# Products of ones ahead of the first weights, modulation rows at the end of the first block, and the gate product split around the gate logits

## The reference, cut to what matters

```python
mod = (silu(c) @ wmod).reshape(2, 6, 1, 256)
sa, ca, ga, sb, cb, gb = (mod[:, i] for i in range(6))
ga, gb = sign(ga) * max(abs(ga), 0.25), sign(gb) * max(abs(gb), 0.25)
h = layernorm(x) * (1 + ca) + sa
q, k, v = h @ Wq, h @ Wk, h @ Wv
gk = log_sigmoid(h @ Wg1 @ Wg2 + bg2) / 16          # cumulated over each chunk of 64
...
o = o * rsqrt(mean(o * o) + EPS) * norm_w * silu(h @ Wgate)
x = x + ga * (o @ Wo)
h = layernorm(x) * (1 + cb) + sb
x = x + gb * moe(h)
```

## Time and profile before

| | us |
|---|---|
| median of three executions | 387.04 |
| their range | 384.47 to 387.41 |
| the profiled execution, its own time | 386.04 |
| its span, first to last instruction | 384.2 |
| mean granted TensorE clock | 0.994 |

### The profile page before, as it was taken

One profiled execution on the slowest core, in us unless ns is written; L12 is line 12 of the kernel. 1 busy time (PEld: TensorE's weight loads), 2 busy tenths in 40 slices (PEclk: granted clock), 3 DMA queues, 4 the chain that ended last, 5 costly groups with the idle time before them and its releaser, 6 DMA issues.

```text
span 384.2 us, 9939 instructions
## 1 busy us (share of the span) xinstructions
PE 359.4 (94%) x3837; PEld 224.8 (59%) x3838; DVE 239.4 (62%) x578; ACT 144.4 (38%) x303; POOL 146.2 (38%) x252
## 2 busy tenths in 40 slices
PE   2989989997989899699999999999999999999996
PEld 2445655674556556554864564576666666666464
DVE  3068767796778878945286483236555555555386
ACT  3395718642846350335023311113333333332110
POOL 7504203500240062005544046540667777675300
PEclk9999999998999999999999999999999999999999
DMA  7960300000000000039931045242233333311296
GB/s 251 309 201 2 114 3 3 2 5 3 1 2 3 3 2 3 4 114 333 292 101 62 1 113 136 90 140 57 83 112 100 108 102 98 99 56 43 83 352 229
DMA packets 29901, 36.66 MB, mean 95 GB/s; under 512 B 4567, under 2 KB 26530, under 8 KB 29860
## 3 DMA queue, kind: packets, MB, share of 16 engines
q1 hardware_dynamic: 26452, 27.58, 23.9%
q0 software_dynamic: 3408, 8.51, 6.5%
HBM read 23.31 MB, written 13.68 MB: 96 GB/s over the span
## 4 chain that ended last, share of the span: by engine, by line
PE 85%; ACT 6%; DVE 4%; issue 3%; DMA 1%; SPq 0%; DVEq 0%; ACTq 0%
PE at_ps L1815 13%; PE work L1445 10%; PE at_ps L1445 8%; PE work L1494 6%; PE at_ps L1460 6%; PE work L1838 4%; PE work L1460 3%; PE work L1840 3%; PE work L1681 2%; PE work L1631 2%; PE at_ps L1494 2%; PE at_ps L1799 2%; PE at_ps L1528 2%; PE at_ps L1681 2%; PE o_even L1584 1%
## 5 line engine op out<-in xcount | busy, mean ns | idle before, releaser
L656 POOL DMA_INDIRECT ys_tokens<-er_pos,goal_u x39 | 41.8, 1073 | 33.8 <-DVE er_pos L1368 25.6
L1815 PE MATMUL at_ps<-arena 128*128 x156 | 54.5, 472 | 0.0
L627 POOL DMA_INDIRECT xs_sorted<-h2tok,pos_u x32 | 31.8, 993 | 36.9 <-DVE pos_u L992 18.6
L585 POOL TENSOR_TENSOR sq<-sq,sg 128x512 f32<-128x512 f32 x8 | 10.0, 1271 | 92.6 <-issue 92.6
L1815 PEld LDWEIGHTS at_ps<-arena 128*128 128x128 f32 x156 | 26.6, 190 | 14.9 <-issue 6.6
L898 ACT ACTIVATE arena<-at_ps 128x176 f32<-128x176 f32 x39 | 12.4, 317 | 58.8 <-PE at_ps L1815 58.8
L1368 DVE SCALAR_TENSOR_TENSOR er_pos<-work,goal,sq 128x256 f32<-128x256 f32 x39 | 17.2, 480 | 22.0 <-PE work L1845 21.0
L1445 PE MATMUL work<-h2T,sup_sb 128*128 128x512 f32 x56 | 25.7, 598 | 0.0
L1348 DVE TENSOR_TENSOR arena<-at_ps,arena 128x176 f32<-128x176 f32 x39 | 13.3, 341 | 18.4 <-ACT arena L898 15.9
L1195 DVE COPY_PREDICATED arena<-causal,at_ps 128x512 f32<-128x512 uint32 x32 | 20.5, 719 | 5.8 <-PE at_ps L1528 5.8
L1460 PE MATMUL at_ps<-sdn_sb,hs 128*128 128x256 f32 x100 | 22.1, 380 | 0.0
(11 more groups left out here) (281 smaller groups left out, 815.6 us busy)
## 6 DMA issues: line engine op xcount, KB each, us to landing
h2tok<-xs_sorted SPq DMA_DIRECT2D x40, 131.5 KB, 2.1
arena<-ys_tokens SPq DMA_DIRECT2D x8, 512.0 KB, 7.8
arena<-in_e_up SPq DMA_DIRECT2D x8, 352.0 KB, 5.5
x_sb<-in_x SPq DMA_DIRECT2D x4, 512.0 KB, 6.9
out_rows<-x_sb SPq DMA_DIRECT2D x16, 128.0 KB, 4.2
sup_sb<-in_s_up SPq DMA_DIRECT2D x2, 640.0 KB, 4.7
xs_sorted<-state SPq DMA_DIRECT2D x2, 526.0 KB, 15.2
xs_sorted<-state SPq DMA_DIRECT2D x8, 131.5 KB, 3.8
```

Source lines behind the costliest of these rows:

```text
L627: g.indirect_dma_start(out=xs_dram, out_offset=bass.IndirectOffsetOnAxis(ap=pos_u[:, k, t:t + 1], axis=0), in_=h2tok[:, t, :], in_offset=N ...
L656: g.indirect_dma_start(out=ys_dram, out_offset=bass.IndirectOffsetOnAxis(ap=goal_u[:, i:i + 1], axis=0), in_=yout[:, q % 2, u, :], in_offs ...
L1815: ins = t_.matmul(at_ps[2 + u % 2][:, 0:2 * FE], xT[:, u % 2, k * P:(k + 1) * P], eup[:, bass.ds(e, 1), k, :].rearrange("p a n -> p (a n)" ...
```

## The change

- TensorE does 14 matmuls of a 128 x 128 tile of ones with itself into `at_ps0` before it waits for the modulation weights, and 3 more behind the first transposes (`idle_products`). Nobody reads their result. GpSimd writes `ones` first and raises the new semaphore `ones_ready` for them.
- `mod_rows` moves on TensorE from behind the low-rank product to between Q and V's second half in slot 0. ScalarE's eviction of it moves from behind `tT` to between the rows of block 1 and V's second half. Their 1024 KB of weights move on SP behind `wq`.
- G of block 0: its first half stands before the gate logits, its second half behind them. TensorE's wait for `const_pool` is gone.
- Banks: MODC goes to `at_ps2`, and of block 0 V's first half to `at_ps0` and K's first half to `at_ps1` (`FIRST_BANKS`), which nobody holds at that time.

```diff
@@ -67,15 +67,19 @@
          ("LR", 0): 3, ("WO", 1): 1, ("Z", 0): 2, ("Z", 1): 3}
 
 
+FIRST_BANKS = {("V", 0): 4, ("K", 0): 5}
+
+
 TAIL_BANKS = {1: (3, 2), 2: (4, 5), 3: (0, 1), 4: (3, 2), 5: (4,)}
 
 
 def unit_order():
-    units = [(("MODC", 0, 0), 0)]
+    units = [(("MODC", 0, 0), 2), (("XT", 0, 0), BANKS["XT", 0]), (("XT", 0, 1), BANKS["XT", 1])]
     ring = [2]
 
     def put(kind, blk, j):
-        units.append(((kind, blk, j), BANKS[kind, j]))
+        own = FIRST_BANKS if blk == 0 else {}
+        units.append(((kind, blk, j), own.get((kind, j), BANKS[kind, j])))
 
     def turn(*keys):
         for key in keys:
@@ -88,12 +92,16 @@
         for kind, blk, i in FILL.get((s, place), ()):
             part(kind, blk, i)
 
-    for kind, j in (("XT", 0), ("XT", 1), ("LR", 0), ("Z", 0), ("Z", 1)):
-        put(kind, 0, j)
+    put("LR", 0, 0)
+    put("G", 0, 0)
+    put("Z", 0, 0)
+    put("Z", 0, 1)
+    put("G", 0, 1)
     for s in range(NBLK):
         b, h = s - 1, s - 2
-        put("G", s, 0)
-        put("G", s, 1)
+        if s:
+            put("G", s, 0)
+            put("G", s, 1)
         put("V", s, 0)
         if h >= 0:
             put("HT", h, 0)
@@ -330,6 +338,7 @@
             sem(n) for n in ("ld_c", "ld_mod", "ld_wg", "ld_wgate", "ld_wv", "ld_wk", "ld_wq",
                              "ld_wo", "ld_rout", "ld_sh", "ld_ex"))
         xs_zero = sem("xs_zero")
+        ones_ready = sem("ones_ready")
         const_pool, ident_ready, zero_ready, kv_full = sem("const_pool"), sem("ident_ready"), sem("zero_ready"), sem("kv_full")
         modf_ready, mod_stored, ld_rows = sem("modf_ready"), sem("mod_stored"), sem("ld_rows")
         unit_full, modr_full, nmr_ready, ld_modr = sem("unit_full"), sem("modr_full"), sem("nmr_ready"), sem("ld_modr")
@@ -421,8 +430,6 @@
             sp.dma_start(csb[:, :, :], cT).then_inc(ld_c, 16)
             sp.dma_start(wmod_sb[:, :, 0:2 * HID], wmod.rearrange("(k p) n -> p k n", p=P)[:, :, 0:2 * HID]
                          ).then_inc(ld_mod, 16)
-            sp.dma_start(wmod_sb[:, :, 2 * HID:6 * HID], wmod.rearrange("(k p) n -> p k n", p=P)[:, :, 2 * HID:6 * HID]
-                         ).then_inc(ld_modr, 16)
             sp.wait_ge(zero_ready, 4)
             sp.dma_start(wg1_sb[:, :, 0:LOWR], wg1.rearrange("(k p) n -> p k n", p=P)).then_inc(ld_wg, 16)
             for j in range(NPAIR):
@@ -433,6 +440,8 @@
             for w_sb, w, s in ((wgate_sb, wgate, ld_wgate), (wv_sb, wv, ld_wv), (wk_sb, wk, ld_wk),
                                (wq_sb, wq, ld_wq)):
                 sp.dma_start(w_sb[:, :, :], w.rearrange("(k p) n -> p k n", p=P)).then_inc(s, 16)
+            sp.dma_start(wmod_sb[:, :, 2 * HID:6 * HID], wmod.rearrange("(k p) n -> p k n", p=P)[:, :, 2 * HID:6 * HID]
+                         ).then_inc(ld_modr, 16)
             for i in range(1, NBLK):
                 sp.dma_start(x_sb[:, i * TPB:(i + 1) * TPB, :],
                              x[i * BLK:(i + 1) * BLK, :].rearrange("(t p) c -> p t c", p=P)).then_inc(ld_x[i], 16)
@@ -515,6 +524,7 @@
         def _(pool):
             g = nc.gpsimd
             steps = Steps(pool, pool_step)
+            g.memset(ones[:, :], 1.0).then_inc(ones_ready, 1)
             g.memset(wg1_sb[:, :, :], 0.0).then_inc(zero_ready, 1)
             g.memset(wg2_sb[:, :], 0.0).then_inc(zero_ready, 1)
             g.memset(rout_sb[:, :, :], 0.0).then_inc(zero_ready, 1)
@@ -524,7 +534,7 @@
             steps.sync()
             g.affine_select(out=ident[:, :], in_=ident[:, :], compare_op=ALU.not_equal, fill=1.0,
                             base=0, pattern=[[-1, P]], channel_multiplier=1).then_inc(ident_ready, 1)
-            for m in (ones, tri, bd16, causal):
+            for m in (tri, bd16, causal):
                 steps.did(g.memset(m[:, :] if m is not causal else m[:, :, :], 1.0 if m is not bd16 else 1.0 / HEAD))
             steps.did(g.memset(rowreset[:, :, :], 1.0))
             steps.did(g.memset(esil[:, :, FE:ODD0], 0.0))
@@ -814,7 +824,6 @@
             act.wait_ge(modc_ready, 2)
             evac_xT(0)
             evac_low_rank(0)
-            evac_mod_rows()
             z_abs(0)
             for s in range(NBLK + 1):
                 b, h = s - 1, s - 2
@@ -864,6 +873,8 @@
                     silu_tables()
                     fill(s, "norm")
                 if s < NBLK:
+                    if s == 0:
+                        evac_mod_rows()
                     evac_v(s, 1)
                     for gr in range(KC):
                         wait_unit(act, ("KT", s, gr))
@@ -1496,19 +1507,25 @@
                 ins.then_inc(unit_full, 1)
 
 
-            pe.wait_ge(csil_ready, 1)
-            pe.wait_ge(ld_mod, 16)
-            o = begin(("MODC", 0, 0))
-            for w in range(2):
-                for h in range(KC):
-                    for k in range(KC):
-                        c0 = w * HID + h * P
-                        ins = t_.matmul(o[:, (w * KC + h) * BATCH:(w * KC + h + 1) * BATCH], wmod_sb[:, k, c0:c0 + P],
-                                        csil[:, k, :], start=(k == 0), stop=(k == KC - 1))
-            ins.then_inc(unit_full, 1)
-            pe.wait_ge(csilb_ready, 1)
+            def idle_products(n):
+
+                for _ in range(n):
+                    t_.matmul(at_ps[0][:, 0:P], ones[:, :], ones[:, :], start=True, stop=True)
+
+            def mod_cols():
+                pe.wait_ge(csil_ready, 1)
+                pe.wait_ge(ld_mod, 16)
+                o = begin(("MODC", 0, 0))
+                for w in range(2):
+                    for h in range(KC):
+                        for k in range(KC):
+                            c0 = w * HID + h * P
+                            ins = t_.matmul(o[:, (w * KC + h) * BATCH:(w * KC + h + 1) * BATCH], wmod_sb[:, k, c0:c0 + P],
+                                            csil[:, k, :], start=(k == 0), stop=(k == KC - 1))
+                ins.then_inc(unit_full, 1)
 
             def mod_rows():
+                pe.wait_ge(csilb_ready, 1)
                 pe.wait_ge(ld_modr, 16)
                 for k in range(KC):
                     for w in range(4):
@@ -1516,8 +1533,6 @@
                                         wmod_sb[:, k, (w + 2) * HID:(w + 3) * HID], start=(k == 0), stop=(k == KC - 1),
                                         skip_group_check=True)
                 ins.then_inc(modr_full, 1)
-
-            pe.wait_ge(ident_ready, 1)
 
             def score(n, q, j):
 
@@ -1699,20 +1714,24 @@
                                             start=True, stop=True)
                 ins.then_inc(kv_full, 1)
 
+            pe.wait_ge(ones_ready, 1)
+            idle_products(14)
+            pe.wait_ge(ident_ready, 1)
+            mod_cols()
             transpose_x(0)
+            idle_products(3)
             pe.wait_ge(ld_wg, 16 * (NPAIR + 3))
             low_rank(0)
-            mod_rows()
+            pe.wait_ge(ld_wgate, 16)
+            project(("G", 0, 0), wgate_sb, 0, hT)
             gate_logits(0)
-            pe.wait_ge(const_pool, 1)
+            project(("G", 0, 1), wgate_sb, 1, hT)
             for s in range(NBLK + 1):
                 b, h = s - 1, s - 2
                 if b >= 0:
                     pe.wait_ge(kh_ready, 2 * b + 2)
                     pe.wait_ge(qeo_ready, 4 * b + 4)
-                if s < NBLK:
-                    if s == 0:
-                        pe.wait_ge(ld_wgate, 16)
+                if 0 < s < NBLK:
                     for gr in range(KC):
                         project(("G", s, gr), wgate_sb, gr, hT)
                 if b >= 0:
@@ -1762,6 +1781,8 @@
                         pe.wait_ge(ld_wq, 16)
                     for gr in range(KC):
                         project(("Q", s, gr), wq_sb, gr, hT)
+                    if s == 0:
+                        mod_rows()
                     values(s, 1)
                     key_rows(s)
                 if s + 1 < NBLK:
```

## The result

The changed kernel takes 383.28 us (median of 19 executions, 380.0 to 385.79), the kernel before 387.03 (19 executions, 384.47 to 389.03). The ratio is 0.9906 with a 95% interval of 0.9882 to 0.9931: 3.75 us, or 0.9%, faster. The forecast was 382.0 with a range of 380.2 to 385.6. The sign and the place were right, the size was 1.3 us too large.

A forecast was written before the change was run, and what follows sets the result against it. TensorE, busy 94% of the span, and its feeding chains bound the kernel. Head 3.45 + hand-over 1.95 - eviction 0.4 = 5.0 us; 386.04 - 5.0 = 381.0, raised by 1.0 toward the median: 382.0, range 380.2 to 385.6.

The forecast's parts named there:

- Fourteen products: TensorE ahead of MODC: the products of ones end by about MODC's weight landing at 6.84, costing 0 to 0.3 us.
- Rival D: TensorE's queue before MODC: products overrun at 0.47 us a pass, some 6 us slower, 393; chance 0.06.
- MODC warm: First modulation matmuls on TensorE: 16 passes at the raised clock take some 1.85 instead of 3.54 us, saving 1.7.
- Low rank: Block 0's low-rank product on TensorE at the raised clock: 1.11 instead of 1.93 us, saving 0.8.
- Gate logits: Block 0's gate logits on TensorE at the raised clock: 1.13 instead of 1.68 us, saving 0.55.
- Rows out, gate half in: Ahead of the gate logits: modulation rows (1.71 us) leave, four gate-product passes (near 1.75) enter; net 0.
- The hand-over: Block 0's V and K no longer wait for the silu, so VectorE's second K product starts earlier; saves 1.95 us.
- Rival E: K still reaches VectorE late, so the 1.95 us fails: gain 3.05, time 384.0; chance 0.08.
- The moved eviction: ScalarE's eviction of the modulation rows, now between next block's row writes and V's eviction, costs 0.4 us.
- Total at the landmark: Start of the second block's low-rank product: 5.0 us earlier, near 32.5 instead of 37.54.
- rival B: Clock falls back in thin work between the products and gate product: 1.7 us lost, gain 3.3, time 383.7; chance 0.17.
- Rival C: Clock not up by 6.84, so MODC and transposes stay cold: gain 1.1, time 385.9; chance 0.14.

The follow-up runs named there:

- rows_early: Changed kernel with the modulation rows, their eviction and their 1 MB load back in the old places: 383.94 us, ratio 0.9935 to the kernel before.
- old_banks: Changed kernel with the first block's V and K back in the banks of G (FIRST_BANKS empty): 386.20 us, ratio 1.0005 to the kernel before.
- the repeat: The changed kernel measured once more, unaltered: 382.99 us, ratio 0.9899 to the kernel before.
- ones_only: Kernel before with only the 14 + 3 products of ones added and `ones` written first: 384.07 us, ratio 0.9938 to the kernel before.
- fill_gaps: Changed kernel with five more products of ones in each of two kinds of later TensorE waits: 387.69 us, ratio 1.0013 to the kernel before.
- no_ones: Changed kernel without any product of ones, keeping the new order: 385.22 us, ratio 0.9969 to the kernel before.
- no_three: Changed kernel without the three products of ones behind the first transposes: 385.98 us, ratio 0.9983 to the kernel before.
- eleven: Changed kernel with 11 instead of 14 products of ones ahead of MODC: 384.52 us, ratio 0.9968 to the kernel before.
- six: Changed kernel with six instead of three products of ones behind the first transposes: 382.90 us, ratio 0.9927 to the kernel before.
- spread: Changed kernel with three more products of ones between MODC and the first transposes, four instead of three behind those: 383.04 us, ratio 0.9909 to the kernel before.
- before_again: The kernel before measured once more, unaltered, for its spread: 386.62 us, ratio 0.9982.

## Why the prediction was right, and where its size was off

Point by point, chain against chain, in the profiled pair:

- *Fourteen products, 0 (0 to 0.3).* They cost 0.48: MODC starts in the chain at 7.32 instead of 6.84. All 28 passes were cold, and 0.22 apart, as the nearest row said, against 0.47 by serial loads. The rise of the clock, taken at 4.3 us behind the first product, came only when the last was done, over 6 us; in rows_early, where the 28 passes took 4.75 us, about half of them were warm, by an estimate from the measured 0.22 us cold and 0.11 warm, and the rise came after about 3 us. Rival D is out: in no profile did they hold MODC back beyond 7.34.
- *MODC warm, 1.7.* 3.54 to 1.68, 1.86. *Transposes, 0.4.* 0.97 to 0.51. *Low rank, 0.8.* 1.93 to 1.07. *Gate logits, 0.55.* 1.68 to 1.11. All within 0.2.
- *Rows out, gate half in, net 0.* 1.71 to 1.92, a loss of 0.2.
- Sum to the end of the gate logits: forecast 3.45, measured 3.20 (ScalarE's absolute value at 18.47 and 15.27).
- *The hand-over, 1.95.* VectorE's second K product moved from 29.20 to 24.11, 5.09, of which 3.20 came from before: 1.89. Rival E is out, and old_banks shows the cause by undoing it: V waits for the silu again. How much of its loss is that wait is said there.
- *The moved eviction, 0.4.* 0.27. The modulation rows on TensorE were hidden, as forecast; old_banks shows that this holds only while TensorE is early.
- *Total at the landmark, 5.0.* 37.54 - 32.71 = 4.83, and 4.81 in the repeat.

The failed step is the last one, where the 4.8 us of the head were carried over to the time in full: the term "386.04 - 5.0 = 381.0". Measured medians give 3.75 and 3.6. With 382.0 forecast and 383.28 measured, the time is nearer to rival B's 383.7 than to the forecast, though the profiled head is the forecast's and not B's. Two things stand between. First, about 0.25 us went in block 1: ScalarE's steps are 4.84 early ahead of TensorE's pauses there and 4.59 behind them. It is not that the pauses are new or longer, since both profiles stand still for 1.45 us in sum; but the changed kernel is stopped twice, and V in two pieces takes 1.35 and 0.92 us where it takes 1.99 in one. Every profile has such pauses between 43 and 56 us, 0.65 us in sum in old_banks and 1.0 to 1.84 in the others; their place moved when the number of instructions ahead did. One lies in V of block 1 in ones_only, rows_early, fill_gaps and the three profiles of the changed kernel, which have 17 products ahead; all lie behind or ahead of V in no_ones, no_three, eleven, six and spread, which have 0, 14, 14, 20 and 21, and in old_banks, which has 17. The trace has loads of 16 KB of instructions in these stretches (41 to 43 us in the changed kernel, 50 to 52 before). That TensorE waits for them is inferred, not shown.

Second, the clock. The prediction had rival B, the fall back, as one case among five with 1.7 us and a chance of 0.17. The falls are not a case that holds or doesn't: they differ from execution to execution, in both kernels. They cost about 0.4 us more in the changed one by the pooled means. Of eleven profiles with products six have a fall in the head (ones_only, rows_early, fill_gaps, six, eleven and spread), five have none (the three of the changed kernel, no_three, and old_banks until its wait for the silu). In the profiled pair it came only behind the head, at 88 to 96 us before and 122 to 128 after. ScalarE's steps are 4.59 us early at 60 us, 6.48 at 97, behind the fall of before, 4.11 at 133, behind the fall of after, and 3.85 from 165 us on, which is the difference of the two spans: the pair happened to pay for one fall each. Rival C was absent: in every profile with products, 14 or 11, MODC was warm or nearly so (1.84 to 2.40 us).

4.83 - 0.25 - 0.4 leaves 4.2; the medians give 3.75 and 3.6. The 0.4 to 0.6 us left are within what the intervals allow, and open.

The prediction also said that less than 3.9 us could not be told from no change. That line was too coarse: the measured 3.75 us falls on the side to which it gave a chance of 0.36, and with 19 executions of each kernel the interval, 2.7 to 4.6 us, is well clear of zero.

## What to carry to other kernels

Work without a result that keeps TensorE busy while it waits for its first data anyway made the thin, serial head of this kernel warm: MODC took 1.92 us instead of 3.54 in ones_only, and the time fell by 2.4 us by itself. Too little of it loses the gain (11 products instead of 14 lost two thirds of it, none of three instead of three nearly all), and too much in the wrong place costs (fill_gaps); six instead of three made no difference clear of noise. The mean granted clock over many executions tells this where one profile doesn't (0.9854 in no_three, whose profile has no fall in the head). Work that is hidden in a gap, as the modulation rows were, is on the path again once its engine is late (1.00 us of the chain in old_banks). Before crediting a head start to the whole, look at how often the clock falls between there and the end, and whether the fall's price differs between the two kernels.

## What the runs showed of the hardware that was not expected

- Behind a wait of 3.43 us in front of V the granted clock was 0.66 over 20 to 25 us (old_banks), which is about 1.8 of the 4.25 us that the undone bank choice cost at the landmark. Behind waits of 1.72 and 1.69 us at the same place (before, ones_only) V was warm.
- Six passes of 0.11 us in a wait of 1.3 us changed the mean clock of the whole kernel from 0.992 to 0.985 when they were taken away. In which places it fell more often is open.
- The first load's landing is not fixed. MODC's wait ended at 6.84, 6.74, 6.92 and 6.96 in before, eleven, spread and old_banks, but at 7.98 in rows_early and 8.20 in before_again, both with the 1 MB load right behind it. So have before and ones_only, where MODC started at 6.84 and 6.58; in the ten profiles with the load moved it started by 7.34 at the latest. Two late landings out of four are few; that the moved load also protects MODC's weights was not tested by itself.
- TensorE stands still with nothing to wait for between 43 and 56 us in every profile, 0.65 to 1.84 us in sum, in one or two places that move with the number of instructions ahead.
